# A fused image-and-text block on one core: one product for the key and query angles, residual rows on ScalarE, new orders of work

## What is computed

```
h = concat([cls, patches @ W.T + b], 1) + pos;  h = concat([h, txt], 1)
x = layernorm(h)
key_phase, query_phase = tanh(x @ Wk + bk) * pi, tanh(x @ Wq + bq) * pi      # 32 planes
V = x @ Wv + bv
total = sum over sets s of softmax(set_weights)[s] *
        Re( (cumsum over rows of exp(i key_phase) V) * exp(-i query_phase) ).sum(planes of s)
gate = sigmoid(x @ Wg + bg)
total = gate * total + (1 - gate) * sigmoid(pos_weight) * (the same with position phases)
h = h + (x + (total / sqrt(8 (row + 1))) @ Wo + bo)
y = layernorm(h)
h = h + silu(y @ sw1) * (y @ sw3) @ sw2 + (the best 2 of 64 experts, at most 256 tokens each, weighted)
```

## Time and profile before

| | us |
|---|---|
| median of three runs | 1766.22 |
| profiled execution | 1764.47 |
| its span, first to last instruction | 1762.7 |
| first token product | 33.97 |
| last token product of the pair loop | 1406.80 |
| last scatter | 1499.37 |

### The profile page before, as it was taken

The page is one execution under the profiler, slowest core; times in us unless marked ns, Lnnn a source line. Parts: engine busy times, 40 slices in busy tenths (PEclk is TensorE's granted clock), DMA queues, the critical chain, the costliest instruction groups (busy, mean ns, idle before and its releaser), DMA issues. The chain is left out here.

```text
span 1762.7 us, 34557 instructions
## 1 busy us (share of the span) xinstructions
PE 1569.5 (89%) x9606; PEld 1162.9 (66%) x9606; DVE 1511.0 (86%) x6004; ACT 1101.5 (62%) x1869; POOL 1226.0 (70%) x1162
## 2 busy tenths in 40 slices
PE   2799999999999999999999999999999982676662
PEld 1577777777777777777777777777777761455551
DVE  2589999999999999999999999999999983687761
ACT  2877777777777777777777777777777631111110
POOL 0117777777777777777777777777777777588888
PEclk9899999999999999999999999999999995798885
DMA  9866766666666666666666666666666201576653
GB/s 172 226 160 141 136 135 130 128 122 126 118 115 114 112 111 111 108 108 108 108 108 110 109 107 107 107 109 108 110 108 106 57 17 34 96 114 99 98 79 33
DMA packets 259956, 194.19 MB, mean 110 GB/s; under 512 B 65513, under 2 KB 239268, under 8 KB 259656
## 3 DMA queue, kind: packets, MB, share of 16 engines
q1 hardware_dynamic: 206008, 173.72, 52.3%
q0 software_dynamic: 51200, 17.87, 8.5%
q10 hardware_dynamic: 2576, 0.60, 0.4%
HBM read 84.84 MB, written 83.73 MB: 96 GB/s over the span
## 5 line engine op out<-in xcount | busy, mean ns | idle before, releaser
L556 POOL DMA_INDIRECT slot_rows<-xs,slot x768 | 823.6, 1072 | 219.5 <-issue 219.5
L549 POOL TENSOR_TENSOR rs<-ve,neg_half 128x6 f32<-128x6 f32 x128 | 172.0, 1343 | 245.8 <-DVE ve L1219 245.8
L615 ACT ACTIVATE img<-img 84x980 f32<-84x980 f32 (+1 forms) x192 | 341.7, 1781 | 0.5 <-DMA img<-img 0.4
L832 PE MATMUL bank<-img,w_tok 126*128 126x392 f32 (+1 forms) x640 | 224.0, 497 | 10.9 <-DMA img<-img 10.9
L596 POOL DMA_INDIRECT out_rows<-img,etok x128 | 199.5, 1559 | 29.7 <-issue 29.7
L832 PEld LDWEIGHTS bank<-img,w_tok 126*128 126x128 f32 (+1 forms) x640 | 117.9, 192 | 83.9 <-issue 13.4
L668 ACT ACTIVATE xs<-h,nb,rs 128x128 f32<-128x128 f32 x384 | 154.7, 481 | 28.5 <-DVE nb L1279 28.5
L913 PE MATMUL bank<-a_t,v 128*128 128x325 f32 (+2 forms) x768 | 167.0, 353 | 1.4 <-DVE a_t L1273 1.4
L895 PE MATMUL bank<-pos_a,v 128*128 128x325 f32 (+2 forms) x768 | 167.6, 353 | 0.0
L684 ACT ACTIVATE xh<-h,nb,rs 128x128 f32<-128x128 f32 x384 | 154.0, 482 | 3.6 <-DVE nb L1279 3.6
L913 PEld LDWEIGHTS bank<-a_t,v 128*128 128x128 f32 (+1 forms) x768 | 130.1, 190 | 28.2 <-issue 1.9
(11 more groups left out here) (192 smaller groups left out, 3669.8 us busy)
## 6 DMA issues: line engine op xcount, KB each, us to landing
img<-in_x SPq DMA_DIRECT2D x384, 150.1 KB
img<-img SPq DMA_DIRECT2D x256, 160.8 KB
img<-img SPq DMA_DIRECT2D x128, 128.6 KB
out_rows<-fin SPq DMA_DIRECT2D x128, 128.0 KB
slot_rows<-xs,slot POOLq DMA_INDIRECT x768
slot_rows<-init_rows SPq DMA_DIRECT2D x16, 540.0 KB, 5.4
img<-slot_rows SPq DMA_DIRECT2D x32, 270.0 KB, 3.3
h<-in_txt SPq DMA_DIRECT2D x64, 128.0 KB, 2.7
```

What stands on the lines that cost most here:

```text
L549: g.tensor_tensor(out=rs[:, q.u], in0=ve[:, q.u], in1=neg_half[:, :], op=ALU.pow).then_inc(s_rs, 1)
L556: g.indirect_dma_start(out=slots_d, out_offset=bass.IndirectOffsetOnAxis(ap=slot[0:nt, q.x, r, part:part + 1], axis=0), in_=xs[0:nt, q.x, ...
L615: a.activation(cols[:, b0:b0 + nb, :], raw[:, q.u, :].rearrange("p (t b) -> p b t", b=P)[:, b0:b0 + nb, :], ACT.Copy)\
L832: ins = mm(bank[:, 4, 0:2 * PATCHES], w_tok[r, m, :], xk[r, k.u, :, m, :], start=(m == 0), stop=(m == SHIFT - 1))
```

## The change

- **Key and query angles.** One weight tile of 128 columns holds Wk twice and Wq twice (`wkq[:, 0]`); for the second image the halves are exchanged (`wkq[:, 1]`). One product for each image gives keys and queries of that image in the two halves of a bank (banks 2 and 3). The query waves then lie in the other half of the partitions than the keys, and ScalarE moves them (`moved_queries`), with the set weight as its scale. `scaled_query` goes; the row norm moves to the mask (`maskn`), and the constants `mask` and `invn` go.
- **Residual.** VectorE's sum of rows and normalized rows becomes six ScalarE operations on the rows, with the normalization's bias and its scale plus one. VectorE makes the scale plus one (`one_more`).
- **Lists.** Each engine's list has a new order, and pairs are at most four bodies back (`p1` to `p4`). TensorE's body now begins with `logits`, and has `transpose_1`, the angles, `values` and all that follows one body after the token product. The third and fourth columns turns of pair 1 no longer stand ahead of the setup's end.
- **Banks and waits.** Most steps have other banks (`project` and `counts` now both use bank 0, so `project` waits for `v_cnt`; tokens and token rows bank 5, values 6 and 7). Many waits go; a few come, all shown below.

The diff, cut to its core (of the changed bodies of ScalarE, TensorE and VectorE only the new lines):

```diff
--- before.py
+++ after.py
...
-for _n, _w in (("ident", 128), ("below", 128), ("mask", 2 * L), ("maskn", 2 * L), ("invn", L), ("iota", CAP),
+for _n, _w in (("ident", 128), ("below", 128), ("maskn", 2 * L), ("iota", CAP),
...
-        wk = sb("wk", [D, 2 * HF])
-        wq = sb("wq", [D, 2 * HF])
-        bk_col = sb("bk_col", [128, 1])
-        bq_col = sb("bq_col", [128, 1])
+        wkq = sb("wkq", [D, 2, 4 * HF])
+        bkq = sb("bkq", [128, 2])
...
-        wn = sb("wn", [128, L])
...
             def body(k):
-                if k.back(-1).runs():
-                    text(k.back(-1))
-                if k.back(-1).runs():
-                    spread(k.back(-1), 1)
-                if k.back(-3).runs():
-                    wait(sp, S["a_d0"], k, -1)
-                    wait(sp, S["a_d1"], k, -1)
-                    wait(sp, S["a_d2"], k, -1)
-                    load(k.back(-3))
-                if k.back(3).runs():
-                    store(k.back(3))
-                if k.back(-2).runs():
-                    wait(sp, S["pe_tok"], k.back(-2), 2)
-                    spread(k.back(-2), 0)
-                    spread(k.back(-2), 2)
+                n4 = k.back(-4)
+                n3 = k.back(-3)
+                n2 = k.back(-2)
+                p2 = k.back(2)
+                if n2.runs():
+                    spread_0(n2)
+                if n4.runs():
+                    if not first(n4):
+                        load(n4)
+                if n2.runs():
+                    text(n2)
+                if n3.runs():
+                    spread_1(n3)
+                    spread_2(n3)
+                if p2.runs():
+                    store(p2)
...
             def body(k):
-                if k.back(2).runs():
-                    rstd(ve2, rs2, k.back(2), S["v_ve2"], S["p_rs2"])
+                p2 = k.back(2)
+                p3 = k.back(3)
+                p4 = k.back(4)
+                if p4.runs():
+                    scatter(p4, 1)
+                if p2.runs():
+                    rstd_2(p2)
+                if p4.runs():
+                    scatter(p4, 2)
                 if k.runs():
-                    rstd(ve1, rs1, k, S["v_ve1"], S["p_rs1"])
-                if k.back(4).runs():
-                    scatter(k.back(4), (1, 2, 3, 4, 5))
-                if k.back(3).runs():
-                    wait(pool, S["v_slot"], k, 3)
-                    wait(pool, S["v_meta"], k, 3)
-                    if first(k.back(3)):
-                        pool.wait_ge(s_init, 16 * (SLOTS // 1024 + 1))
-                    wait(pool, S["p_go"], k, 4)
-                    g.tensor_tensor(out=spare[:, 2:3], in0=neg_half[:, 0:1], in1=neg_half[:, 1:2], op=ALU.add)\
-                        .then_inc(S["p_go"], 1)
-                    scatter(k.back(3), (0,))
-            steps(pool, body)
+                    rstd_1(k)
+                if p4.runs():
+                    scatter(p4, 3)
+                    scatter(p4, 4)
+                    scatter(p4, 5)
+                if p3.runs():
+                    ready(p3)
+                    scatter(p3, 0)
+            steps(body, 0, 4)
...
+            def residual(k):
+                act.wait_ge(S["v_rp"], k.count())
+                for i in range(2 * NT):
+                    ins = a.activation(hbo[:, k.u, i, :], h[:, k.u, i // NT, i % NT, :], ACT.Identity,
+                                       bias=nb1[:, k.u, i:i + 1], scale=rp1[:, k.u, i:i + 1])
+                ins.then_inc(S["a_hb"], 1)
...
+            def angles_0(k):
+                act.wait_ge(S["pe_k0"], k.count())
+                a.activation(ph_t[:, 0, :], bank[:, 2, 0:L], ACT.Tanh, bias=bkq[:, 0:1])
+            def angles_1(k):
+                act.wait_ge(S["pe_k1"], k.count())
+                a.activation(ph_t[:, 1, :], bank[:, 3, 0:L], ACT.Tanh, bias=bkq[:, 1:2]).then_inc(S["a_th1"], 1)
...
+            def moved_queries(k):
+                act.wait_ge(S["a_sin"], k.count())
+                for s in range(2):
+                    to, at = slice(64 * s, 64 * s + 64), slice(64 - 64 * s, 128 - 64 * s)
+                    ins = a.activation(qs[to, k.u, :], kq[at, k.u, s, :], ACT.Identity, scale=wcol[at, 4:5])
...
             def body(k):
+                n2 = k.back(-2)
+                p1 = k.back(1)
+                p2 = k.back(2)
+                p3 = k.back(3)
+                if p1.runs():
+                    residual(p1)
+                    distance(p1)
+                    waves(p1)
+                if p3.runs():
+                    score_parts(p3)
+                if p1.runs():
+                    moved_queries(p1)
                 if k.runs():
                     image_rows(k)
+                if p1.runs():
+                    gate(p1)
+                if p2.runs():
+                    normal_2(p2)
+                if n2.runs():
+                    if not early(n2, 1):
+                        turn_columns_1(n2)
+                if p2.runs():
+                    columns_2(p2)
                 if k.runs():
                     normal_1(k)
+                if n2.runs():
+                    if not early(n2, 2):
+                        turn_columns_2(n2)
+                if p2.runs():
+                    logit_columns(p2)
+                    shared_silu(p2)
                 if k.runs():
                     columns_1(k)
+                if n2.runs():
+                    if not early(n2, 0):
+                        turn_columns_0(n2)
                 if k.runs():
+                    angles_0(k)
+                if p2.runs():
+                    logit_rows(p2)
                 if k.runs():
+                    angles_1(k)
+            steps(body, -2, 3)
...
             def scores(y):
-                pe.wait_ge(S["a_sin"], y.count())
-                pe.wait_ge(S["v_qn"], y.count())
-                wait(pe, S["a_h"], y, -1)
-                wait(pe, S["a_lg"], y, 2)
-                pe.wait_ge(S["a_thk"], y.count())
+                pe.wait_ge(S["a_g"], y.count())
                 for i, (t0, _) in enumerate(TILES):
                     for s in range(2):
                         r = slice(64 * s, 64 * s + 64)
-                        b = 6 - 2 * s
+                        b = (6, 4)[s]
                         dst = (bank[:, b, 0:L], bank[:, b + 1, 0:L - TILE], bank[:, b + 1, L - TILE:L])[i]
-                        ins = mm(dst, kq[r, y.u, 0, t0:t0 + TILE], qn[r, y.u, t0:L], start=(i < 2), stop=(i != 1),
+                        ins = mm(dst, kq[r, y.u, s, t0:t0 + TILE], qs[r, y.u, t0:L], start=(i < 2), stop=(i != 1),
                                  skip_group_check=True)
                 ins.then_inc(S["pe_sc"], 1)
...
             def project(y):
                 pe.wait_ge(S["v_tot"], y.count())
-                wait(pe, S["a_sl"], y, 1)
+                wait(pe, S["v_cnt"], y, 2)
                 for s in range(2):
                     for i, (t0, _) in enumerate(TILES):
-                        ins = mm(bank[:, 3 + s, i * D:(i + 1) * D], tot[:, s, t0:t0 + TILE], wo[:, :], start=True, stop=True)
+                        ins = mm(bank[:, s, i * D:(i + 1) * D], tot[:, s, t0:t0 + TILE], wo[:, :], start=True, stop=True)
                 ins.then_inc(S["pe_wo"], 1)
             def values(k):
...
+            def angles_1(k):
+                mm(bank[:, 3, 0:L], wkq[:, 1, :], x_t[:, 1, :], start=True, stop=True).then_inc(S["pe_k1"], 1)
+            def angles_0(k):
                 pe.wait_ge(S["a_xt"], k.count())
+                mm(bank[:, 2, 0:L], wkq[:, 0, :], x_t[:, 0, :], start=True, stop=True).then_inc(S["pe_k0"], 1)
...
             def body(k):
+                p1 = k.back(1)
+                p2 = k.back(2)
+                p3 = k.back(3)
+                p4 = k.back(4)
+                if p3.runs():
+                    logits(p3)
+                if p4.runs():
+                    counts(p4)
+                if p3.runs():
+                    shared_1b(p3)
+                    shared_1a(p3)
+                if p1.runs():
+                    transpose_1(p1)
+                if p2.runs():
+                    project(p2)
+                if p3.runs():
+                    shared_3b(p3)
+                    shared_3a(p3)
+                if p1.runs():
+                    angles_0(p1)
+                if p3.runs():
+                    logit_rows(p3)
+                if p1.runs():
+                    angles_1(p1)
                 if k.runs():
                     token(k)
+                    if first(k):
+                        position_products()
+                if p1.runs():
+                    values(p1)
+                    gates(p1)
                 if k.runs():
                     token_rows(k)
+                if p3.runs():
+                    shared_out(p3)
+                if p1.runs():
+                    position_out_0(p1)
+                    scores(p1)
+                    position_out_1(p1)
+                if p2.runs():
```

(133 more changed lines are left out.)

495 lines of the change are left out of this document (158 added, 337 removed).

## The result

The changed kernel takes 1737.09 us (median of 4 runs, 1735.91 to 1737.79) against 1765.73 for the kernel before beside it: a ratio of 0.9836, 95% interval 0.9819 to 0.9853. The forecast was 1738. Its profiled span is 1736.0 us, against 1762.7.

The account below looks back on a forecast made before the run. TensorE was taken as the bound, losing some 0.3 us per body to a full VectorE. Bodies -24.0, start +1.3 and end -4.3 made -27 from 1764.47: 1737.5, forecast 1738, range 1716 to 1762 (the forecast case's own 1720 to 1752).

Parts of the forecast that it names:

- the scatters' end: At the kernel's end, GpSimd's chain of scatters was forecast to end near 1474 us.
- no rival: New waits take the gain back, 1758 (22%); ScalarE becomes the bound, 1788 (11%); merged product at face value, 1705 (6%).
- The merged product: In TensorE's body, full-width key and query products replace half products: gain 0.10 us, bounds 0 and 0.62.
- the lower bound: Body of 21.1 us, if 0.1 at each remaining half-width step and 0.2 of first position products go too.
- The waits for VectorE: TensorE's waits for a full VectorE go, per body: 0.16 us for the masks and 0.14 for `both`.
- The 60 bodies: Pair loop from token 3 to token 63: 0.40 us less per body, -24.0 in all.
- Start and end: Start, to token 3: +1.3 us (-3 to +5); end, after the last token product: -4.3 (-8 to +2).
- The rival that ScalarE becomes the bound: Rival 2, 11%: ScalarE's remaining waits make a body 22.2 us, and the time 1788.
- estimate of 0.46: ScalarE's moves of the queries: 0.46 us each by the Trainium skill's figures; the prediction took 0.5.

Follow-up runs that it names:

- the doubled ones: The changed kernel with ScalarE's two moves of the queries made twice: 1741.52 us, 4.4 more than the changed kernel.

## Why the prediction came out right, and where it did not

The time and the scatters' end are those forecast, the body lies within its bounds (21.18, for 21.1 to 21.76), TensorE is the bound, the added work of ScalarE is hidden, and no rival came true. But the terms of the body were sized wrongly, and a loss was missed.

1. **The merged product, 0.10 in the forecast, was worth 0.34 in the body** (angles 1.24 to 1.10, `project` -0.09, `values` -0.11), and 0.30 by the run that undoes it alone. I had compared the halves with each other and put a price only on what lay inside the step. That a neighbour pays 0.1 could be seen in the trace of before at a shared product: 0.64 ahead of the logits, 0.55 elsewhere. I used this in the lower bound, for the half-width steps that remain, and left it out of the sum for those that go. The runs give the price here: 0.30 to 0.34 us for a visit.
   The rule for it stands in the Trainium skill (TensorEngine Tiling (Array Packing), section Tiling Modes): changing the tiling mode, not only the tile, drains TensorE. I had cited that section for the speedup of two tiles and had left out this line of it. The runs agree with it, in that the price goes by visits; a drain as such is shown by none.
2. **The waits for VectorE, 0.30 in the forecast, were 0.12 where they can be taken away** (21.76 to 21.65 without the scaled query). In the changed kernel the group of shared out, scores, position and phase products gains only 0.08, and no part of it need be a wait. `shared_out` takes 1.34 where it took 1.44 ahead of the scores (64 rows), and the scores 0.03 less. The two position products, 1.27 and 1.11 before, take 1.20 and 1.21 with the scores between them, 0.03 more together, and the phase products 0.02 more. So the first position product did fall into its forecast of 1.1 to 1.2, but the steps on both sides of the scores now pay, where the counts stood behind them before. How much of the 0.08 is a wait that went and how much a price that moved, no run separates.
3. **What I hadn't costed:** the logits, also 64 columns wide, now stand at the counts, and the shared products around them take 0.12 less.
4. **The 60 bodies** were forecast at 0.40 each, 24.0. They gave 0.60 each, against the 21.78 that they took on average before, and lost 9.3 once, at the first scatter, for which GpSimd waited 18.1 us. I had walked SP's list for its buffers and not for the clearing of the slots. The change issues its last part a body later, at 126.13 where it was 106.14. Before, the first scatter found it done at 118.36; now GpSimd is there at 113.28 and waits until 131.42. With the clearing earlier the kernel is 7.0 faster.
5. **Start and end:** +2.95 and -2.7, for +1.3 and -4.3, both within their bounds. ScalarE has a large part in the start: without the residual's six operations pair 3 is 3.6 earlier. I had put pair 1's three column turns, 5.1 us, behind the setup as new; before, only two of them stood ahead of it (3.30 us at 29.57), and pair 0's image rows start 2.2 later, at 46.04 for 43.86.
6. **ScalarE and VectorE.** 20.02 and 20.05 for 19.9 and 19.8. Of VectorE's, 0.46 is the wait told of below, so its work is 19.6. The moves take 0.57 each, for 0.5. The rival that ScalarE becomes the bound was further off than its 11% say: 20.94 us of work in 21.18 hold nobody.

The forecast's total was right within 1 us because errors cancelled: the 60 bodies' own length gave 12.2 us more than forecast (36.2 for 24.0), and 9.3 lost once, 1.7 at the start and 1.6 at the end took it back.

## To carry to other kernels

Work out the cost of a step of TensorE with its neighbours: compare the same instructions behind and ahead of different tile shapes, and count the visits to a shape, not the products in it; put steps of one shape side by side, or make them full width if the time is the same. After an order of lists is changed, ask of every one-off job (clearing, setup, first loads) whether it comes later than it did, or its first user earlier. Work taken off an engine that isn't the bound brings only what the bound waited for it: 0.12 us a body for the scaled query, which stood ahead of the masks, and nothing for the residual, though that was twice as long. And look at the start by itself: each run that gave ScalarE more work paid 1.6 to 5.7 us there with the same body.

## What the runs showed of the hardware

- A visit of TensorE to products with 64 columns of weights costs 0.30 us (body 21.48 against 21.18), two visits with the same products 0.65 (21.83).
- ScalarE's two moves to other partitions don't overlap as its other operations do. In order of time, two of the changed kernel's lists:

```profile
802.39 2.40 ACT L705 ACTIVATE xh<-h,nb,rs 128x128 f32<-128x128 f32 x6
...
816.02 1.14 ACT L764 ACTIVATE qs<-kq,wcol 64x325 f32<-64x325 f32 x2
```

  Six operations of 482 ns take 2.40 us together, 0.5 less than one behind the other; two of 565 ns take 1.14, 0.57 each, and so do the doubled ones, four in 2.30. By the Trainium skill (ScalarE: Activation LUTs, What ACT_TABLE_LOAD costs) successive ones overlap by 93 ns, from which the prediction had its estimate of 0.46; the six agree with it, the two don't. Why, no run shows.
- A length in a trace can hold a wait. VectorE's 128x6 operation `rp` ahead of `weigh_sets` is recorded with 0.63 us in one body and 0.16 in another:

```profile
802.70 0.83 DVE L1362 SCALAR_TENSOR_TENSOR gpos<-gt,bank 128x650 f32<-128x650 f32 x1
803.45 0.63 DVE L1376 TENSOR_SCALAR rp<-rs 128x6 f32<-128x6 f32 x1
804.00 0.83 DVE L1367 SCALAR_TENSOR_TENSOR gsets<-gt,bank 128x650 f32<-128x650 f32 x1
...
1332.95 0.16 DVE L1376 TENSOR_SCALAR rp<-rs 128x6 f32<-128x6 f32 x1
1333.50 0.83 DVE L1367 SCALAR_TENSOR_TENSOR gsets<-gt,bank 128x650 f32<-128x650 f32 x1 [0.38 <-PE bank L939]
```

  It has 0.62 or 0.63 in 29 of 63 bodies, and 0.16 to 0.18 in the others. From 168 us on the next operation starts 0.53 to 0.56 behind it in all of them, and where it is short the trace names the wait: for the phase products. So the 0.46 between the two lengths is read as this wait. VectorE's busy time in a body then is 19.6, and not 20.05.
- Six products of float32 with 64 moving columns take 1.28 us, with 128 moving columns 1.34.
